# Graph passes: SyncE fetches six or seven tiles' rows one at a time, GpSimd gathers the others

## The reference

```
h = x @ W_in + b_in                                   # layer 3
for l in range(3):
    agg = segment_sum(h[src], dst) / deg
    h = relu(agg @ W_agg[l] + h @ W_self[l] + b_hid[l])
x = layernorm(x + h @ W_out + b_out)

def rgcn(x):                                          # layer 4, twice, relu between
    msg = einsum(comp[edge_type], (x @ basis)[src])
    norm = 1 / count of edges with the same (dst, edge_type)
    return segment_sum(msg * norm, dst) + x @ root + bias
x = layernorm(x + rgcn(relu(rgcn(x))))
```

## Time and profile before

| what | value |
|---|---|
| median of 3 runs | 7177.48 us (7175.35 to 7201.99) |
| profiled execution, its own time | 7132.51 us |
| its span | 7130.8 us |
| GpSimd busy | 63% of the span |
| PE busy | 61% |
| VectorE busy | 44% |
| granted TensorE clock, mean | 0.781 of full speed |
| the five graph passes | 3820 to 7131 us |

### The profile page before, as it was taken

One profiled execution on the slowest core, in us unless ns is written; L12 is line 12 of the kernel. 1 busy time (PEld: TensorE's weight loads), 2 busy tenths in 40 slices (PEclk: granted clock), 3 DMA queues, 4 the chain that ended last, 5 costly groups with the idle time before them and its releaser, 6 DMA issues. The chain is left out here.

```text
span 7130.8 us, 75257 instructions
## 1 busy us (share of the span) xinstructions
PE 4317.0 (61%) x20054; PEld 2955.9 (41%) x20055; DVE 3165.0 (44%) x6539; ACT 1916.6 (27%) x4343; POOL 4465.6 (63%) x4304
## 2 busy tenths in 40 slices
PE   1000588888766666668896455455477767775555
PEld 1000365656534444445674333233344434443333
DVE  5040345544446888878644222222244433333443
ACT  2630355555424555446461000000000000000000
POOL 2677566666546888746313666666566646665666
PEclk6555788888778899989997676767688878887766
DMA  3112122222105666657103445454455544443333
GB/s 85 46 41 54 55 65 67 66 66 67 42 25 178 210 210 213 189 168 215 43 0 122 145 147 140 147 147 146 129 170 176 176 114 133 131 134 97 97 97 87
DMA packets 466880, 826.73 MB, mean 116 GB/s; under 512 B 146229, under 2 KB 316182, under 8 KB 460057
## 3 DMA queue, kind: packets, MB, share of 16 engines
q0 software_dynamic: 209808, 566.12, 27.9%
q1 hardware_dynamic: 256777, 256.98, 11.3%
HBM read 664.90 MB, written 157.90 MB: 115 GB/s over the span
## 5 line engine op out<-in xcount | busy, mean ns | idle before, releaser
L1349 POOL DMA_INDIRECT p_rows<-table,idx_s x1320 | 1292.0, 979 | 773.7 <-issue 372.2
L1394 PE MATMUL p_psA<-p_rows,p_hot 128*128 128x256 bf16 (+1 forms) x4840 | 895.0, 349 | 602.1 <-DMA p_rows<-table,idx_s 401.7
L1394 PEld LDWEIGHTS p_psA<-p_rows,p_hot 128*128 128x128 bf16 (+1 forms) x4840 | 622.1, 134 | 856.2 <-issue 714.3
L585 POOL DMA_INDIRECT p_space<-h_table,p_space x440 | 451.6, 1026 | 289.5 <-issue 126.9
L571 POOL DMA_INDIRECT rec_s<-p_rec_out,p_row_s x416 | 429.8, 1033 | 283.0 <-ACT p_rec_out L696 138.3
L1349 POOL DMA_INDIRECT p_rows<-rel_table,edge_d x440 | 433.8, 986 | 254.0 <-issue 126.2
L655 PE MATMUL p_psW<-p_wf,p_upto 128*128 128x256 f32 x1760 | 480.1, 434 | 183.9 <-DVE p_upto L815 163.3
L376 POOL DMA_INDIRECT rec_d<-edge_d,norm x416 | 426.4, 1025 | 238.2 <-issue 125.3
L1557 POOL DMA_INDIRECT p_rows<-rel_table,edge_d x440 | 437.8, 995 | 219.3 <-issue 129.9
L1423 ACT ACTIVATE sums<-p_psA,inv_degree 128x256 f32<-128x256 f32 x75 | 35.6, 474 | 1850.7 <-DMA p_locs<-loc_rows 963.0
L1777 POOL DMA_INDIRECT p_kg<-kv_table,edge_d x440 | 425.1, 966 | 165.2 <-issue 111.6
(11 more groups left out here) (354 smaller groups left out, 8749.8 us busy)
## 6 DMA issues: line engine op xcount, KB each, us to landing
v_sorted<-p_kg SPq DMA_DIRECT2D x110, 512.0 KB
p_val<-v_sorted SPq DMA_DIRECT2D x110, 512.0 KB
rel_table<-p_o SPq DMA_DIRECT2D x50, 1024.0 KB
p_rows<-table,idx_s POOLq DMA_INDIRECT x1320
p_space<-rec_s SPq DMA_DIRECT2D x110, 136.0 KB
p_locs<-loc_rows SPq DMA_DIRECT2D x110, 128.0 KB, 4.3
p_rows<-rel_table,edge_d POOLq DMA_INDIRECT x880
p_rec_out<-edge_attr SPq DMA_DIRECT2D x103, 128.0 KB
```

The costliest lines, as they stand in the source:

```text
L585: pool.indirect_dma_start(msg[q][:, u, :], None, table, bass.IndirectOffsetOnAxis(ap=rec_i[q][:, u, S_IDX:S_IDX + 1], axis=0))\
L1349: pool.indirect_dma_start(rows[q][:, u, :], None, table, bass.IndirectOffsetOnAxis(ap=idx(n * U + u), axis=0))\
L1394: step = pe.matmul(psA[:, bass.ds(at[u], D)], hot[q][:, u, :], rows[q][:, u, c * D:(c + 1) * D], start=False, stop=(c == terms - 1), skip_ ...
```

## The change

The class `Singles` picks, from `Posts`' places, one tile about every 3.2 blocks, at least 11 groups after SyncE can have begun with it: tiles 104, 156, 208, 260, 312, 384 and 436 in passes 1, 2 and 4; 112, 164, 216, 268, 320 and 392 in pass 3; 100, 152, 204, 256, 308, 380 and 432 in the last. GpSimd leaves these tiles out. SyncE brings their rows, ROWS = 40 in each block's slot ahead of the block's store, each row with a DMA of its own. The row's place is read from SBUF into a register, four places with one load; the places themselves (128 words) are brought from DRAM a tile ahead. The rows go into two buffers outside the ring (`g.spare`: two SBUF tensors whose contents are no longer needed). PE waits for `brought` before it uses such a tile. In the last pass PE's loop becomes straight code, since a tile's number must be known.

```diff
+def straight(total, ring, stages):
+
+    ahead, behind = max(lead for lead, _ in stages), min(lead for lead, _ in stages)
+    for k in range(-ahead, total - behind):
+        for lead, step in stages:
+            if 0 <= k + lead < total:
+                step(Turn((k + lead) // ring, (k + lead) % ring, ring))
...
+class Singles:
+    HELD, ROWS, MARGIN, SPREAD_OVER = 2, 40, 6, 3
+
+    def __init__(self, g, plan, table, freed):
+        self.g, self.listed, self.table, self.lists, self.tiles = g, plan.listed, table, plan.banks[32:33, :], []
+        self.high = table.shape[0] - 1
+        for i in range(g.NB * Singles.ROWS // P):
+            slot = (P * (i + 1) - 1) // Singles.ROWS
+            begun = freed[slot - 1] if slot else 0
+            tile = (begun + -(-Singles.ROWS // (2 * U)) + Singles.MARGIN) * U
+            if tile < g.NT:
+                self.tiles.append(tile)
+        self.number = {tile: i for i, tile in enumerate(self.tiles)}
+
+    def gathers_before(self, n, ring):
+
+        return sum(u + m * U not in self.number for m in range(n % ring, n + 1, ring) for u in range(U))
+
+    def note(self, sp, i, listed):
+        if i < len(self.tiles):
+            c = i % Singles.SPREAD_OVER * P
+            sp.dma_start(self.lists[:, c:c + P], self.listed(self.tiles[i]).rearrange("p o -> o p"),
+                         allow_slow_non_contiguous=True).then_inc(listed[i % Singles.SPREAD_OVER], 16)
+
+    def bring(self, nc, sp, slot, held, brought, listed, summed):
+
+        for r in range(slot * Singles.ROWS, min((slot + 1) * Singles.ROWS, len(self.tiles) * P), U):
+            i, p = divmod(r, P)
+            if r == 0:
+                self.note(sp, 0, listed)
+            if p == 0:
+                self.note(sp, i + 1, listed)
+                sp.wait_ge(listed[i % Singles.SPREAD_OVER], 16 * (i // Singles.SPREAD_OVER + 1))
+                if i >= Singles.HELD:
+                    sp.wait_ge(summed, self.tiles[i - Singles.HELD] // U + 2)
+            at = nc.values_load_multi_w_load_instructions(
+                self.lists[:, i % Singles.SPREAD_OVER * P + p:i % Singles.SPREAD_OVER * P + p + U], engines=[SPE],
+                min_val=0, max_val=self.high,
+                skip_runtime_bounds_check_because="places of nodes' rows in a table that holds all nodes")[1]
+            for u in range(U):
+                sp.dma_start(held[i % Singles.HELD][p + u:p + u + 1, :], self.table[bass.ds(at[u], 1), :])\
+                    .then_inc(brought[i % Singles.HELD], 16)
...
                 for k in range(NB):
+                    singles.bring(core.nc, sp, k, held, brought, listed, summed)
                     b = block_of_rank(core.nc, g, plan, SPE, k)
...
                     for u in range(U):
+                        if n * U + u in singles.number:
+                            continue
                         pool.indirect_dma_start(rows[q][:, u, :], None, table,
...
-                        pe.wait_ge(gathered[q], (n // ring + 1) * (16 * U))
+                        pe.wait_ge(gathered[q], 16 * singles.gathers_before(n, ring))
                         for u in range(U):
+                            i, row = singles.number.get(n * U + u), rows[q][:, u, :]
+                            if i is not None:
+                                pe.wait_ge(brought[i % Singles.HELD], 16 * P * (i // Singles.HELD + 1))
+                                row = held[i % Singles.HELD][:, :]
...
-                pipelined(pe, groups, ring, [(0, total)])
+                straight(groups, ring, [(0, total)])
```

More of the change, by code:

```diff
@@ L1247, in after, with place_of @@
         return self.at.get(n, ())
+    def place_of(self, part, k):
+        return next(n for n, parts in self.at.items() if (part, k) in parts)
     def turned_for(self, part, k):
@@ L1315, in fused_pass @@
         gathered = [s.sem(f"gathered{q}") for q in range(ring)]
+        singles = Singles(g, plan, table, [posts.place_of(Posts.SPREAD, k) for k in range(NB)])
+        held = [a.bitcast(BF16 if halves else F32)[:, 0:terms * D] for a in g.spare]
+        brought, listed = ([s.sem(f"{name}{q}") for q in range(n)] for name, n in (("brought", Singles.HELD),
+                                                                               ("listed", Singles.SPREAD_OVER)))
         stored = [s.sem(f"stored{q}") for q in range(OUTS)]
@@ L1390, in _ @@
                         pe.wait_ge(hotted, n + 1)
-                        pe.wait_ge(gathered[q], (n // ring + 1) * (16 * U))
+                        pe.wait_ge(gathered[q], 16 * singles.gathers_before(n, ring))
                         for u in range(U):
+                            i, row = singles.number.get(n * U + u), rows[q][:, u, :]
+                            if i is not None:
+                                pe.wait_ge(brought[i % Singles.HELD], 16 * P * (i // Singles.HELD + 1))
+                                row = held[i % Singles.HELD][:, :]
                             for c in range(terms):
-                                step = pe.matmul(psA[:, bass.ds(at[u], D)], hot[q][:, u, :], rows[q][:, u, c * D:(c + 1) * D],
+                                step = pe.matmul(psA[:, bass.ds(at[u], D)], hot[q][:, u, :], row[:, c * D:(c + 1) * D],
                                                  start=False, stop=(c == terms - 1), skip_group_check=True)
@@ L1528, in last_pass @@
         gathered = [s.sem(f"gathered{q}") for q in range(ring)]
+        singles = Singles(g, plan, table, [posts.place_of(Posts.TURN, k) for k in range(NB)])
+        held = [a.bitcast(F32)[:, 0:D] for a in g.spare]
+        brought, listed = ([s.sem(f"{name}{q}") for q in range(n)] for name, n in (("brought", Singles.HELD),
+                                                                               ("listed", Singles.SPREAD_OVER)))
         stored = [s.sem(f"stored{q}") for q in range(2)]
@@ L1569, in total @@
                     pe.wait_ge(hotted, t.n + 1)
-                    pe.wait_ge(gathered[t.q], t.i * (16 * U) + 16 * U)
+                    pe.wait_ge(gathered[t.q], 16 * singles.gathers_before(t.n, ring))
                     for u in range(U):
-                        step = pe.matmul(psA[:, bass.ds(at[u], D)], hot[t.q][:, u, :], rows[t.q][:, u, :],
+                        i, row = singles.number.get(t.n * U + u), rows[t.q][:, u, :]
+                        if i is not None:
+                            pe.wait_ge(brought[i % Singles.HELD], 16 * P * (i // Singles.HELD + 1))
+                            row = held[i % Singles.HELD][:, :]
+                        step = pe.matmul(psA[:, bass.ds(at[u], D)], hot[t.q][:, u, :], row,
                                          start=False, stop=True, skip_group_check=True)
                     step.then_inc(summed, 1)
-                pipelined(pe, groups, ring, [(0, total)])
+                straight(groups, ring, [(0, total)])
             @block.scalar
@@ L2315, in graph_layers @@
         w_p = sb("w_p", [P, KT, D])
+        g.spare = [g.blk_d[:, :], w_p[:, :, :].rearrange("p k n -> p (k n)")]
         with nc.sbuf_tensor("score", [P, g.NT, H], F32) as score, \
```

4 lines of the change are left out of this document (added).

## The result

| | before | after |
|---|---|---|
| median of the runs (first chip) | 7185.44 us (7175.35 to 7201.99) | 8205.73 us (8195.72 to 8215.04) |
| ratio | | 1.142, 95% interval 1.140 to 1.143 |
| span of the profiled execution | 7130.8 us | 8195.6 us |
| granted TensorE clock, mean | 0.781 | 0.746 |

The change makes the kernel 14% slower on the chip of the first measurement: 1020 us in the medians, 1065 us between the two profiled spans. (The median of before is that of four runs here, three stood ahead of the prediction.) The forecast was 7840 us, "SyncE falls behind", with a range to 8500.

The account below looks back on a forecast made before the run. GpSimd issuing gathers, 1.25 us each, was taken to bound the passes. Three passes at +226 us (+678) less 16 in passes 3 and 4 give +662 on 7132.5, 7794; with 45 for timed runs 7840 us, range 7110 to 8500.

Parts of the forecast that it names:

- The forecast case: Graph passes: SyncE's row DMAs make it fall behind; 7840 us, likeliest range 7250 to 8500, chance 0.50.
- Rival A: Graph passes: SyncE keeps up, rows below 0.62 us, 42.5 us off GpSimd's path; 7135 us, chance 0.37.
- quiet price: SyncE's cost per row where nothing disturbs it: 0.56 us, making a block's slot 23.2 us of 25.5.
- The row's price in passes 1 and 2: SyncE's row DMA there, also in the last pass: 0.87 us, geometric middle between 0.56 and 1.36.
- the state feeds on GpSimd's stream: SyncE's slow instructions: when SyncE is late, GpSimd stands still longer and SyncE recovers, so no more than 0.87 us a row.
- the split by passes: Rows at 0.56 us in passes 3 and 4, at 0.87 us in passes 1, 2 and the last.
- the case that the prediction named: Stated sign: if passes 3 and 4 are slowed too, the row price is right and the split wrong.
- my own formula: Slowed pass: 22.4 blocks of 35.6 us plus 2.6 of 25.5 make 864 us against 638, +226 us.
- the 42.5 us for the gathers: GpSimd in the five passes: 34 of 2200 gathers dropped at 1.25 us each, 42.5 us less issue.
- Rival C: SyncE keeps up, but dropped gathers fall in ring waits, or rows crowd the gathers; 7145 to 7180 us, chance 0.13.
- The slot's remainder: SyncE's part of each block besides the rows: the block's own store with its load, some 0.8 us.
- The page's rule: SyncE's copy instructions at 512 cycles, 0.43 us: a row 0.72 us, a block 29.6, some 7630 us; not used in the sum.

Follow-up runs that it names:

- const1: Changed kernel with each of the 40 row DMAs from a constant place, no register work on SyncE; 7212.7 us, 1.0023 of the kernel before on chip D.
- silent: Changed kernel with GpSimd gathering only the first ring of groups in each pass, SyncE still fetching 40 rows a slot; 6430.8 us, single run on chip B.

## Why the prediction was right, and where not

- **The forecast case.** Right: SyncE falls behind, its stores and held tiles come late, GpSimd's waits grow from 75 to 92 us a pass (beyond 1.25 us a gather) to 238 to 357. Rival A's threshold of 0.62 us a row was the right question. Its 25.5 us a block came from a trace in which PE stalls; on B and C a block takes 22.0 to 22.5 us without the tiles, and by that the threshold is (22.5 - 0.8) / 40 = 0.54 us. The quiet price of 0.56 us is already over it. I had read the cover from a kernel that was itself disturbed.
- **The row's price in passes 1 and 2.** 0.87 us forecast, 0.867 and 0.868 measured; a slot 35.6 forecast, 36.1 and 36.5 measured. The reason given, that the state feeds on GpSimd's stream and SyncE recovers when GpSimd stands, is what the sorted distances show. That the geometric middle hit to the second digit is luck: the ends were 0.56 and 1.36.
- **What failed: the split by passes.** "passes 3 and 4 at 0.56 us" were 0.90 and 0.95, and the last 0.98. I had priced the two passes at 16 us gained together; they lost 143 + 224 = 367. This is 383 of the missing 403 us (1065 of the spans against 662), and the case that the prediction named: the price right, the split wrong. I took the split from the durations of SyncE's stores, never over 0.341 us in passes 3 and 4. But each of those 50 stores stands alone behind a wait, and so does the register operation ahead of L1542, at 0.046 us in the worst pass too. A lone instruction behind a wait doesn't measure what a run of instructions costs. What did run through those passes was PE's program, and the trace of before shows GpSimd waiting there somewhat more than elsewhere: beyond 1.25 us a gather, 89 us in pass 4 and 92 in pass 3 (641 us from first to last gather), for 77 and 78 in passes 1 and 2. Had I asked which passes have ring waits, and not which have slow stores, I would have priced all five alike: (864 - 638) x 5 = +1130 us by my own formula, near the 1065.
- **The other terms.** Passes 1 and 2 lost 184 and 190 us for 226. The formula let 2.6 blocks without rows follow at 25.5 us each, 66 us. In pass 1 SyncE's last row was issued at 4652.2 us, GpSimd had issued the pass's last gather at 4616.9, PE's last sum ended at 4656.4, and the next pass's first gather came at 4669.0. So the tail took some 17 us, because the last blocks' rows were gathered while SyncE was still late. In the last pass 308 for 226: the row at 0.98. Of the 42.5 us for the gathers, which the prediction priced but which only passes 3 and 4 of its sum contain, nothing shows on A, where SyncE is the bound; on B they are there (42.1 us; that it is so near is luck, with an interval of 31 to 48).
- **Rival C.** On B there is no sign of it. On D its first half is what `const1` shows in passes 1 and 2: GpSimd's ring waits grew by 9 and 10 us, as much as seven gathers. For its second half, rows that crowd the gathers, no run speaks. The rows went as one packet each: the profile of the changed kernel has 12160 packets of 1536 bytes on the queue that SyncE's DMAs use, for 9600 before, and passes 1 to 3 fetch 2560 rows; so no row was spread over several engines. Packets of that size took 0.07 to 0.08 us in the mean in the passes, rows and stores together, half of the 0.15 us that the prediction took from the gathers' queue.
- **The slot's remainder.** The block's own store with its load was taken as 0.8 us. In `silent` it is 24.1 - 40 x 0.566 = 1.5 us in passes 1 and 2 and 25.1 - 40 x 0.561 = 2.7 in the last, with two stores. The load of four places takes 0.558 us on SyncE, not the 0.332 of PE's; the rest of the row was cheaper by as much, and the 0.56 us held.
- **The page's rule.** The Trainium skill ("DMA: Bandwidth & Descriptors", the table of sequencer cycles in the section "Why a DMA increments its semaphore by 16 and not by 1") gives 512 cycles for a copy instruction of the generations before the newest, by the prediction's estimate 0.43 us at 1.2 GHz. No run agrees: the row's own DMA instruction has a median of 0.223 to 0.228 us on A and on C. Its sum, 7630 us, lies further from the 8206 than the sum by the rows.

## What to carry to other kernels

Before moving work to an idle queue, price it as a run of instructions beside the work that will run then, and take that price from an engine which does issue many in a row there; single instructions behind waits can look cheap where a run of them is not (0.341 us at most for the stores of passes 3 and 4, but 0.90 and 0.95 us a row). Compare it with the block time that the kernel would have without its own disturbances, since that is the cover that counts. And where a price moves with the neighbour's activity, measure on more than one chip: the same edit was 14% slower on one and 0.5% on another.

## What the runs showed of the hardware

- The same kernel takes 7185 and 7197 us on two measurements and 6483 to 6489 on the others, with the granted clock of the profiled runs at 0.78 and 0.82. On A and D many of SyncE's instructions last 0.70 us or a multiple of it, or stand that far apart (a register operation of 0.037 us goes up to 1.4 us). Among the rows' instructions and their loads in the changed kernel, 2444 durations and gaps lie within 0.02 us of 0.70, 1.40 or 2.10 us on A, and 29 on C. What sets a chip apart in this way, no run shows.
- On A and D SyncE's instructions get dearer the longer GpSimd has issued indirect DMAs in a row (0.73 us a row in the first 5 us, 1.96 after 15 to 20 us, on A) and are back at 0.62 us when the last of these began over 3 us ago.
- On A and D PE stalls too where nothing is named: 242 us ahead of the sums' matmuls in the kernel before on A, up to 13.5 us at a time, and 5 us on C. The 6.61 us in the earlier trace rows are one of them. On D it is 157 us in passes 1 to 4, and 348 when SyncE issues its rows beside it.
